# A decoder layer on one core: the first norm of the next batch on ACT, written as scale and shift by rows, with its load and its statistics moved forward

## What is computed

```
h1 = layernorm(x);  z = softmax over the rows of (h1 @ W_A.T / 4)          # 16 heads
x  = x + (Toeplitz matrix of each head's z, lower triangle) @ (h1 @ W_V.T) @ W_O.T + b_O
h2 = layernorm(x);  x = x + softmax(causal, h2 @ WQ @ (ctx @ WK).T / 16) @ (ctx @ WV)
h3 = layernorm(x);  x = x + shared experts(h3) + the top 2 of 16 routed experts(h3), weighted
```

## Time and profile before

| | |
|---|---|
| median of 3 runs | 619.41 us |
| profiled execution, own time | 620.24 us |
| its span, first to last instruction | 618.5 us |
| PE matmul busy | 560.0 us (91%) |
| DVE busy | 464.0 us (75%) |
| ACT busy | 229.1 us (37%) |
| POOL busy | 167.3 us (27%) |
| mean granted PE clock | 0.981 |
| iteration 5, from its first to the next one's first Toeplitz product | 64.5 us |

### The profile page before, as it was taken

How to read it: one execution, slowest core, us unless ns; L and a number is a source line. 1 busy time by engine, 2 the same in 40 slices (tenths; PEclk the granted TensorE clock), 3 DMA queues, 4 the chain that set the end, 5 groups by cost and what they waited for, 6 DMA issues and landing times. The chain is left out here.

```text
span 618.5 us, 13541 instructions
## 1 busy us (share of the span) xinstructions
PE 560.0 (91%) x5116; PEld 376.6 (61%) x5116; DVE 464.0 (75%) x1148; ACT 229.1 (37%) x447; POOL 167.3 (27%) x189
## 2 busy tenths in 40 slices
PE   3678697899989999999989999999999999999897
PEld 2346455656657656766666666766586667666455
DVE  4686557767888779887988788878877777777754
ACT  3654242533334433343333333343233432342322
POOL 2233033031341233321242134123322232223114
PEclk9979778999999999999999999999999999999999
DMA  8882943589134963189326922593339524500250
GB/s 294 303 270 97 338 158 127 163 199 359 56 81 114 270 237 102 43 165 338 84 60 136 315 94 70 132 290 125 102 85 263 170 68 107 103 1 2 66 109 34
DMA packets 90672, 94.74 MB, mean 153 GB/s; under 512 B 28160, under 2 KB 76160, under 8 KB 90368
## 3 DMA queue, kind: packets, MB, share of 16 engines
q1 hardware_dynamic: 90624, 94.09, 53.6%
HBM read 75.66 MB, written 12.12 MB: 142 GB/s over the span
## 5 line engine op out<-in xcount | busy, mean ns | idle before, releaser
L601 POOL TENSOR_TENSOR mid<-gated,mid 128x512 f16<-128x512 f32 x72 | 83.7, 1162 | 276.6 <-ACT mid L741 276.6
L741 ACT ACTIVATE mid<-gated 128x512 f16<-128x512 f32 x72 | 45.1, 626 | 99.7 <-DVEq L1026 99.6
L142 PE MATMUL wide<-w_d,mid 128*128 128x256 f16 x288 | 78.6, 273 | 0.1
L144 PE MATMUL wide<-w_d,mid 128*128 128x256 f16 x288 | 78.5, 273 | 0.0
L143 PE MATMUL wide<-w_d,mid 128*128 128x256 f16 x288 | 78.5, 273 | 0.0
L1007 DVE SCALAR_TENSOR_TENSOR gated<-gated,score 128x512 f32<-128x512 f32 x72 | 48.8, 678 | 26.4 <-ACT gated L736 25.1
L142 PE MATMUL score<-h3T,w_gu 128*128 128x512 f16 x160 | 60.7, 380 | 1.6 <-DVEq L122 1.4
L143 PE MATMUL rows<-h3T,w_gu 128*128 128x512 f16 x160 | 60.7, 380 | 0.0
L142 PE MATMUL rows<-h3T,w_gu 128*128 128x512 f16 x160 | 60.7, 379 | 0.0
L144 PE MATMUL score<-h3T,w_gu 128*128 128x512 f16 x160 | 60.7, 379 | 0.0
L144 PE MATMUL rows<-h3T,w_gu 128*128 128x512 f16 x160 | 60.7, 379 | 0.0
(11 more groups left out here) (211 smaller groups left out, 1374.5 us busy)
## 6 DMA issues: line engine op xcount, KB each, us to landing
toep<-z_scratch SPq DMA_DIRECT2D x16, 2048.0 KB, 18.3
stage<-comb_scratch SPq DMA_DIRECT2D x32, 512.0 KB, 7.9
x_in<-in_xr SPq DMA_DIRECT2D x8, 512.0 KB, 11.1
x_bo<-in_x SPq DMA_DIRECT2D x8, 512.0 KB, 12.6
qT<-q_scratch SPq DMA_DIRECT2D x7, 512.0 KB, 3.7
vx<-v_scratch SPq DMA_DIRECT2D x7, 512.0 KB, 5.1
out<-x_out SPq DMA_DIRECT2D x7, 512.0 KB, 3.0
q_scratch<-stage SPq DMA_DIRECT2D x6, 512.0 KB, 5.6
```

The lines of the kernel that those rows point to most:

```text
L142: pe.matmul(out, stationary[0], moving[0], start=start, stop=False, **kw)
L144: return pe.matmul(out, stationary[1], moving[0], start=False, stop=stop, **kw)
L601: pool.tensor_tensor(mid_slot(j, 1, late), gate_slot(j, late), mid_slot(j, 0, late), ALU.subtract).then_inc(mid_split.sem, 1)
L741: act.activation(mid_slot(j, 0, late), gate_slot(j, late), ACT.Copy).then_inc(mid_hi.sem, 1)
```

## The change

SP issues the load of x of batch `it + 1` as the first thing of iterations 2 to 6. DVE takes the statistics of all 4 blocks directly behind the gate of slice 0, ahead of x_res. POOL makes the reciprocal deviation of batch `it + 1` behind `part_mid` of slice 0 and ahead of that of the second norm, and two more small instructions: minus_mean = -mean, and shift = minus_mean * rstd. ACT, behind tanh of slice 1, makes x_in = rstd * x_in + shift with 4 instructions (`norm_x`), in place of DVE's `normalise`. The split of h1 moves from slice 6 to slice 3 on ACT and to slice 4 on DVE. Iterations 0 and 1 keep DVE's `normalise`.

```diff
@@ sync: iteration
+                if d and n:
+                    load_x(it + 1, 1 if c == 6 else None)
                 if m and d:
                     move_mix(it - 1)
...
                 if d:
                     spread_comb(it, it - 2)
-                if d and n:
-                    load_x(it + 1, 1 if c == 6 else None)
@@ gpsimd
+            def make_shift(b):
+
+                pool.tensor_scalar(minus_mean[:], mean_var[0][:, :, 0], -1.0, None, ALU.mult).then_inc(mean_turned.sem, 1)
+                pool.wait_ge(mean_turned.sem, mean_turned.at(b, 1))
+                pool.wait_ge(rstd_done[0].sem, rstd_done[0].at(b, 1))
+                pool.tensor_tensor(shift[:], minus_mean[:], rstd[0][:], ALU.mult).then_inc(shift_made.sem, 1)
@@ gpsimd: iteration
+                if n and d:
+                    reciprocal_deviation(it + 1, 0)
+                    make_shift(it + 1)
                 if m:
                     reciprocal_deviation(it - 1, 1)
...
-                    if n and j == (4 if d else 5 if m else 1):
+                    if n and not d and j == (5 if m else 1):
                         reciprocal_deviation(it + 1, 0)
@@ scalar
+            def norm_x(b):
+
+                act.wait_ge(shift_made.sem, shift_made.at(b, 1))
+                for c in range(C):
+                    last = act.activation(x_in[:, c], x_in[:, c], ACT.Identity, bias=shift[:, c:c + 1],
+                                          scale=rstd[0][:, c:c + 1])
+                last.then_inc(x_normed.sem, 1)
             def part_h1(b):
-                act.wait_ge(h_ready[0].sem, h_ready[0].at(b, 2))
+                act.wait_ge(x_normed.sem, x_normed.at(b, 1))
@@ scalar: iteration
                         tanh(it, it - 2, j)
+                        if n and j == 1:
+                            norm_x(it + 1)
...
                         part_prob(it, it - 1, j - AHEAD)
+                        if n and d and j == 3:
+                            part_h1(it + 1)
...
-                    if n and d and j == 6:
-                        part_h1(it + 1)
@@ vector: iteration
                     gate(it, it - 2, 0)
+                if n and m and d:
+                    x_statistics(it + 1)
...
-                        if d and j in (3, 4):
-                            x_statistics(it + 1, range(2 * (j - 3), 2 * (j - 3) + 2))
+                        if d and j == 4:
+                            part_h1(it + 1)
...
-                        if j == (5 if d else C + AHEAD):
+                        if not d and j == C + AHEAD:
                             normalise(it + 1, it, 0, x_in, x_in)
-                        if d and j == 6:
-                            part_h1(it + 1)
```

More of the change, by code:

```diff
@@ L246, in decoder_layer @@
         rstd = [sb(f"rstd{n}", [P, C]) for n in range(3)]
+        minus_mean = sb("minus_mean", [P, C])
+        shift = sb("shift", [P, C])
         loads = [
@@ L337, in decoder_layer @@
         h_ready = [sig(f"h_ready{n}", 2, 1) for n in range(3)]
+        mean_turned = sig("mean_turned", 1, -3)
+        shift_made = sig("shift_made", 1, -3)
+        x_normed = sig("x_normed", 1, -3)
         x_biased = sig("x_biased", 1)
```

## The result

Over 18 runs the changed kernel takes 623.24 us (621.33 to 624.53) and the kernel before 619.72 us (617.35 to 621.05): ratio 1.0057, 95% interval 1.0043 to 1.0071, or +3.5 us. The forecast was +2.2 us, 621.6.

What follows compares the result with a forecast made beforehand. The prediction took PE to bound the kernel, its products filling 62.30 of iteration 5's 64.50 us. Iterations 4 to 6 at -0.1 each and 2 and 3 at +1.3 each were rounded to +2.2: 621.6 us, range 615.5 to 627.

Steps and rivals of the forecast that it cites:

- The load, price 0: Start of the iteration: issuing the load of x ahead of the mix's transposes costs nothing.
- Behind gate 0, 1.4 us: DVE, iterations 4 to 6: statistics added ahead of x_res make the scores start 1.4 us later.
- Rival 3: Second norm: idle spots hide the statistics and POOL's added work is covered too; 615 us, faster; chance 0.13.
- Slice 4 and 5: DVE's split takes 1.2 us in slice 4, holds POOL's low part, and PE pays 0.4 us per iteration.
- Rival 1: Slice 4: POOL gets the port before the split, costing 0.9 for 0.4 us; 624.1 us, slower; chance 0.15.
- Slices 5 to 9, -1.0 and -0.86: With less work on DVE, PE's waits for h3 (1.0 us) and before the logits (0.86 us) go.
- rival 2: Slices 6 to 9: another release holds DVE back, so 1.86 us isn't regained; 631 us, slower; chance 0.07.
- POOL's detour in iterations 2 and 3: First norm's rstd and shift, 1.9 us, delay the second norm's rstd and h2; scores start 2.75 us later overall.
- Rival 4: Iterations 2 and 3: only POOL's detour is hidden, by the gate of slice 1; 619.3 us, no change; chance 0.10.
- The sum: Whole kernel: -0.3 us for iterations 4 to 6 and +2.6 for 2 and 3, rounded to +2.2.
- The forecast "within 0.5%": Whole kernel: the time stays within 0.5% (3.1 us) of the kernel before; chance 0.50.

Runs made afterwards that it cites:

- e2: The kernel before with only the load of x moved to the start of the iteration; 622.73 us, ratio 1.0062.
- e5: The changed kernel with SP holding the load of x in iteration 3 until half of PE's Toeplitz products are done; 619.76 us, ratio 1.0010.
- e3: e2 plus the statistics of x behind the gate of slice 0 and the first norm's rstd ahead of the second's; 628.70 us, ratio 1.0150.
- e6: The changed kernel with the second norm's rstd first on POOL and norm_x moved to slice 3 on ACT; 621.27 us, ratio 1.0035.
- e4: The kernel before with only the normalise of x moved to ACT (slice 6), POOL's shift in slice 4; 608.04 us, ratio 0.9829.
- e7: e4 with the load of x moved to the start of the iteration; 611.93 us, ratio 0.9870.

## Why the prediction was right in sign and range, and what it had wrong

- **The load, price 0: wrong.** This step failed. "SP loses nothing" and "the 512 KB leave the busier time behind" were true of SP and of the data, but the transfer of PE's instructions was in no step. e2 prices it at 1.0062 alone, e5 takes it out of the changed kernel and leaves 1.0010. In the trace it is 2.8 us in iteration 3 (74.51 - 71.73). Of these 1.4 are the hole (1.59 against 0.20 in e5), and the other 1.4 are added over the next 83 products, most of the 3.41 us at half clock among them.
- **Behind gate 0, 1.4 us: right in iterations 4 to 6.** PE's three gaps at the second norm are 0.2, 0.9 and 0.8 us longer than the products before them need, against one of 0.75 before, and the scores start 22.70 us into iteration 5 in place of 21.41: +1.3. Rival 3, hidden statistics, falls: e3 pays them.
- **Slice 4 and 5: right.** Split 1.2, low part 2.0 forecast, 1.21 and 1.93 found; PE waits 0.4 for x_res, of which a part was there before, unseen. Rival 1 falls.
- **Slices 5 to 9, -1.0 and -0.86: right.** Both waits are gone; rival 2 falls. From the attention block on, iteration 5 gains 2.0 us, 0.2 more than the 1.86, and with the scores 0.1 earlier than forecast it came out 0.3 better (-0.38).
- **POOL's detour in iterations 2 and 3: right, the iteration as a whole too dear.** In iteration 2, where no hole is, the third context unit starts 1.7 us later (1.8 forecast) and the scores 2.6 later (2.75 forecast), so 0.9 comes in between (0.95 forecast); e6 recovers 0.9. Rival 4, the detour hidden, falls with it. Yet the iteration is only +0.78, not +1.3: the attention block costs 0.2 there, not 0.4, and from it on 2.05 us are gained, not 1.86. In iteration 3 of e5, with the load held back, the scores start only 2.35 later.
- **The sum.** Its own terms add up to +2.3 or +2.4 and were put as +2.2. Without the load it would have been 0.78 + about 0.5 (71.73 - 71.24) + 0.11 - 0.38 - 0.41 = about +0.6, and about +0.3 if the 0.3 us are taken off by which iteration 4's gap has grown. That is far less than forecast; with the load it is +3.4. A load priced at nothing and iterations priced too dear brought the total near +2.2 by luck. The forecast "within 0.5%" missed its edge by 0.07%.

The gain was in the change all along: what e4 does alone is worth 10 us. The changed kernel gains the same 2.0 us in slices 5 to 9 of iteration 5, where PE's two late waits for DVE end once DVE has 2.1 us less to do, and pays most of it back at the second norm, where DVE has no slack.

## What to carry to other kernels

Move work off the engine that ends a wait, and leave the order of the rest alone: e4's one move gave 1.7%, and each of the two moves added to it, statistics ahead of a tight chain and load ahead of a dense product stretch, cost 0.4% to 0.9% (e7 against e4, e2, e3 against e2). Before a large load is issued into a stretch in which PE runs many short products, see where the instruction transfers lie in the DMA queues; in these runs one came up to 1.9 us later with the load in front of it. Where a sum comes out right, compare it iteration by iteration before believing its terms.

## What the runs showed of the hardware that was not expected

- PE runs out of instructions. In the five kernels with the load first in iteration 3 (changed, e2, e3, e6, e7) the Toeplitz products stop behind the 172nd of 192, with 1.4 to 2.15 us to the next; in the four others the gap is 0.2 us. The stretch until the stop holds 172 products and 172 weight loads in 4.48 us. The Trainium skill, "Runtime: NRT & Kernel Launch", section "Instruction fetch mechanics", has instructions come in blocks of 16 KB, 256 instructions each, and calls the transfer mostly hidden. The size agrees with the transfer in the queues; that it is hidden these runs contradict.
- The granted clock falls behind such a hole in the changed kernel, e2, e6 and e7: 0.50 for 3.41 us from 191.00 on in the changed kernel, 0.1 us after PE goes on. It is no rule: the gap of 2.53 us before the third context unit of iteration 3 left the clock full in the changed kernel, and in e3 it is the other way round, with the clock full behind the hole of 1.42 us and 0.50 for 3.41 us behind the gap of 2.53. The kernel before is at full clock from 107.5 us on, not from 60: its trace has 0.50 from 69.95 to 83.60 and from 104.08 to 107.49.
- Identity with scale and bias by rows takes 2.08 us for four blocks of 256 columns on ACT, and no table load appears beside it (the trace's only one is at 0.8 us). The prediction's estimate from the Trainium skill, "ScalarE: Activation LUTs", section "What ACT_TABLE_LOAD costs", was 2.06; the trace agrees.
